# Latent attention: the norm in its own block, three groups projected at once, raw copies and GpSimd roots

## The reference, cut to what matters

```python
xn = layernorm(x, ln_x_g, ln_x_b); ln = layernorm(latents, ln_l_g, ln_l_b)   # x: context, latents: layernorm(x)
q = (ln @ Wq)...; kv = concatenate([xn @ Wkv, ln @ Wkv], axis=1)             # 16 heads of 64
qn = rmsnorm(q, qn_g) * scale; kn = rmsnorm(k, kn_g)
sim = einsum('bhid,bhjd->bhij', qn, kn); ... masked; attn = softmax(sim)
out = einsum('bhij,bhjd->bhid', attn, v) ... @ Wout + bout
x = x + tanh(g) * out
```

## Time and profile before

| | us |
|---|---|
| median of 3 runs | 1561.75 (1558.82 to 1564.23) |
| profiled execution, its own time | 1560.97 |
| its span | 1558.9 |
| TensorE busy | 1319.1 (85%), mean granted clock 0.926 |
| VectorE, ScalarE, GpSimd busy | 833.6 (53%), 688.5 (44%), 490.2 (31%) |
| latent attention, start to first exponential | 472.4 to 550.34 |

### The profile page before, as it was taken

One profiled execution on the slowest core, in us unless ns is written; L12 is line 12 of the kernel. 1 busy time (PEld: TensorE's weight loads), 2 busy tenths in 40 slices (PEclk: granted clock), 3 DMA queues, 4 the chain that ended last, 5 costly groups with the idle time before them and its releaser, 6 DMA issues. The chain is left out here.

```text
span 1558.9 us, 19760 instructions
## 1 busy us (share of the span) xinstructions
PE 1319.1 (85%) x7007; PEld 574.6 (37%) x7007; DVE 833.6 (53%) x1386; ACT 688.5 (44%) x1153; POOL 490.2 (31%) x471
## 2 busy tenths in 40 slices
PE   5779687759966699999999999999959976677998
PEld 2214222238952233333333333333326752222443
DVE  3757666362344566655665666566364434632554
ACT  3354434422225256655665666465433434254222
POOL 1013201066610144453553444445416750010000
PEclk9999899769977899999999999999979997797999
DMA  8500400249531000000000000000041123000340
GB/s 229 223 1 0 109 17 1 94 145 381 212 97 60 0 1 1 1 0 1 1 0 1 1 1 0 1 0 1 1 145 40 53 73 114 0 1 1 77 102 13
DMA packets 44267, 85.73 MB, mean 55 GB/s; under 512 B 7646, under 2 KB 27230, under 8 KB 43422
## 3 DMA queue, kind: packets, MB, share of 16 engines
q1 hardware_dynamic: 30124, 70.44, 13.9%
q0 software_dynamic: 4544, 9.32, 2.1%
q10 hardware_dynamic: 9504, 4.72, 1.1%
HBM read 76.56 MB, written 11.04 MB: 56 GB/s over the span
## 5 line engine op out<-in xcount | busy, mean ns | idle before, releaser
L2456 ACT ACTIVATE a_prob<-a_TP 128x512 f32<-128x512 f32 x256 | 138.9, 595 | 121.0 <-PE a_TP L2287 119.2
L2541 DVE TENSOR_REDUCE a_lat<-a_SP 128x2 f32<-128x1024 f32 x128 | 156.0, 1218 | 59.1 <-PE a_SP L2256 59.1
L2652 POOL TENSOR_TENSOR a_acc<-a_prob 128x512 f32<-128x512 f32 x64 | 79.8, 1267 | 303.1 <-ACT a_prob L2456 303.1
L2283 PE MATMUL a_TP<-a_qn,a_kn 64*128 64x512 f32 x512 | 148.0, 642 | 2.9 <-ACT a_prob L2456 2.9
L2298 PE MATMUL a_MS<-a_prob,a_V 128*64 128x512 f32 x512 | 122.7, 599 | 0.2 <-ACT a_prob L2456 0.2
L3109 DVE TENSOR_REDUCE a_nm<-a_A 128x8 bf16<-128x616 f32 x84 | 67.0, 797 | 50.6 <-PE a_A L2829 50.4
L3287 POOL TENSOR_TENSOR a_on<-a_osb,a_rden 128x512 f32<-128x512 f32 x9 | 11.4, 1271 | 242.9 <-ACT a_osb L3001 242.9
L2661 POOL TENSOR_TENSOR a_acc<-a_acc,a_prob 128x512 f32<-128x512 f32 x64 | 79.9, 1270 | 18.4 <-ACT a_prob L2456 18.4
L2656 POOL TENSOR_TENSOR a_acc<-a_acc,a_prob 77x512 f32<-77x512 f32 x64 | 80.2, 1273 | 0.0
L2283 PEld LDWEIGHTS a_TP<-a_qn,a_kn 64*128 64x128 f32 x512 | 40.6, 185 | 105.1 <-issue 75.4
L2456 ACT ACTIVATE a_prob<-a_TP,a_rowneg 77x512 f32<-77x512 f32 x64 | 40.3, 678 | 72.2 <-PE a_TP L2287 72.2
(11 more groups left out here) (493 smaller groups left out, 2854.3 us busy)
## 6 DMA issues: line engine op xcount, KB each, us to landing
ring_w<-in_F_w SPq DMA_DIRECT2D x64, 512.0 KB, 8.7
f_wide<-weight_rows SPq DMA_DIRECT2D x24, 256.0 KB, 5.7
a_maskT<-in_maskT SPq DMA_DIRECT2D x1, 2304.0 KB
a_biasT<-in_biasT SPq DMA_DIRECT2D x1, 2304.0 KB
f_b<-in_F_b SPq DMA_DIRECT2D x1, 2048.0 KB
token_rows<-f_xtok ACTq DMA_DIRECT2D x8, 256.0 KB, 5.9
a_biasQ<-in_biasQ SPq DMA_DIRECT2D x3, 616.0 KB, 5.5
ring_w<-expert_rows SPq DMA_DIRECT2D x6, 256.0 KB, 6.9
```

What stands on the lines that cost most here:

```text
L2283: nc.tensor.matmul(TP[0:n, h, :], keys(h), qn[half(h), r % 4, :], start=True, stop=False)
L2456: nc.scalar.activation(prob[0:n, 2 * k + h, :], TP[0:n, h, :], ACT.Exp, bias=rowneg[0:n, b:b + 1] if k == 0 else 0.0).then_inc(p_ready, 1)
L2541: nc.vector.tensor_reduce(lat[:, g % 2, 2 * u:2 * u + 2], SP[:, :, :], AX.X, ALU.max, negate=True).then_inc(s_used, 1)
L2652: nc.gpsimd.tensor_tensor(acc[:, h, :], prob[:, 2 + h, :], prob[:, 4 + h, :], ALU.add).then_inc(added, 1)
```

## The change

The norm is no longer a block of its own: its five pieces are part of the attention's block, in the order x of batch 0, context, x of batch 1, x of batch 2, x of batch 3, and the last two lie between later work (`centre`, `variance` on TensorE, `square_x`, `scale_x` on ScalarE, `normal` on VectorE). The loads get a semaphore each for what needs them, masks and constants before Wv and Wo. Groups 0, 1 and 2 are projected into three bank pairs (QK, TP, SP). Of groups 1 and 2 and of the context, VectorE copies the raw projection, scaled by the gain, to SBUF (`keep_raw`, `keep_context`), which frees the banks, and GpSimd multiplies by the root there (`root_raw`, `root_context`); group 0 stays as it was, and context 0 is multiplied by VectorE (`norm_context(0)`). Means of the context go to QK in place of SP, so that SP is free for the maxima. Half of the twelve value copies go to ScalarE (`keep_values`). Adding the bias to x moves to GpSimd, behind its casts.

```diff
+context = (c.ctxrep[:, :, 0:SK], cn[:, :], CW, once, 0, TP[:, 1, :], SP[:, 1, :])
+PIECES = [(c.xT[:, b * S:(b + 1) * S], c.xn[:, b * S:(b + 1) * S], S, twice, 2, TP[:, 0, :] if b == 0 else DEN,
+       SP[:, 0, :] if b == 0 else O) for b in range(B)]
+PIECES.insert(1, context)
...
+def raw_bank(g):
+    return (QK, TP, SP)[g] if g < 3 else QK
...
+def squares_of(g):
+    return V[:, 1, 2 * g - 2:2 * g, :] if g in (1, 2) else sq[:, :, :]
...
+def roots_of(g):
+    return on[:, 0:2, :] if g == 1 else rn[:, :, :]
...
-        nc.tensor.matmul(QP[:, :], Wq[:, p * P:(p + 1) * P], c.xn[:, b * S:(b + 1) * S],
+        bank = raw_bank(g)
+        nc.tensor.matmul(bank[:, 0, :], Wq[:, p * P:(p + 1) * P], c.xn[:, b * S:(b + 1) * S],
                          start=True, stop=True).then_inc(q_ready, 1)
-        if g:
+        if g >= 3:
             pe.wait_ge(k_normed, g)
-        nc.tensor.matmul(KP[:, :], Wk[:, p * P:(p + 1) * P], c.xn[:, b * S:(b + 1) * S],
+        nc.tensor.matmul(bank[:, 1, :], Wk[:, p * P:(p + 1) * P], c.xn[:, b * S:(b + 1) * S],
                          start=True, stop=True).then_inc(k_ready, 1)
...
         if i:
-            pe.wait_ge(c_normed, i)
+            pe.wait_ge(c_squared, i)
+            pe.wait_ge(c_kept, i)
...
     def mean_context(i):
+        pe.wait_ge(first_q, i + 2)
+        pe.wait_ge(first_k, i + 2)
         pe.wait_ge(c_squared, i + 1)
...
+    def first_values(i):
+        bank = (QP, KP)[i % 2]
+        if i == 0:
+            pe.wait_ge(v_in, 16)
+        if i < 2:
+            pe.wait_ge((q_normed, k_normed)[i], 1)
+        else:
+            pe.wait_ge((first_q, first_k)[i % 2], i // 2)
+        if i >= QT:
+            pe.wait_ge(c_clipped, i // 2 - 1)
...
+        dve.wait_ge(q_squared, g + 1)
+        nc.vector.tensor_scalar(qn[:, g, :], raw_bank(g)[:, 0, :], cv[:, 0:1], None,
+                                ALU.mult).then_inc(raw_kept, 1)
+        dve.wait_ge(k_squared, 2 * g + 2)
+        nc.vector.tensor_scalar(kn[:, g, :], raw_bank(g)[:, 1, :], vec[:, 5:6], None,
+                                ALU.mult).then_inc(raw_kept, 1)
...
+        dve.wait_ge(c_squared, i + 1)
+        nc.vector.tensor_scalar(knc[:, 2 * i:2 * i + 2, :], TP[:, :, 0:CW], vec[:, 5:6], None,
+                                ALU.mult).then_inc(c_kept, 1)
...
     def norm_context(i):
         dve.wait_ge(c_rms, i + 1)
-        nc.vector.scalar_tensor_tensor(out=knc[:, 2 * i:2 * i + 2, :], in0=TP[:, :, 0:B * SK],
-                                       scalar=vec[:, 5:6], in1=prob[:, 6:8, 0:B * SK], op0=ALU.mult,
-                                       op1=ALU.mult).then_inc(c_normed, 1)
+        dve.wait_ge(c_kept, i + 1)
+        nc.vector.tensor_tensor(knc[:, 2 * i:2 * i + 2, :], knc[:, 2 * i:2 * i + 2, :], c_clip(i),
+                                ALU.mult).then_inc(c_normed, 1)
...
+    def root_raw(g):
+        pool.wait_ge(ms_rms, g + 1)
+        pool.wait_ge(raw_kept, 2 * g)
+        nc.gpsimd.tensor_tensor(qn[:, g, :], qn[:, g, :], roots_of(g)[:, 0, :], ALU.mult)\
+            .then_inc(q_normed, 1)
+        nc.gpsimd.tensor_tensor(kn[:, g, :], kn[:, g, :], roots_of(g)[:, 1, :], ALU.mult)\
+            .then_inc(k_normed, 1)
...
+    nc.gpsimd.tensor_scalar(c.xT[:, :], c.xT[:, :], cv[:, 1:2], None, ALU.add).then_inc(prep, 1)
...
```

More of the change, by code:

```diff
@@ L2153, in latent_attention @@
[L2153 to L2157, removed]
+        vec_in, masks_in, prep = sem("vec_in"), sem("masks_in"), sem("prep")
+        qk_in, v_in, blk_in, o_in = sem("qk_in"), sem("v_in"), sem("blk_in"), sem("o_in")
@@ L2210, in _, with centre, variance @@
             @block.tensor
             def _(pe):
+                def centre(i):
+                    src, _, w, _, _, bank, _ = PIECES[i]
+                    if i >= 3:
+                        pe.wait_ge(n_normed, i)
+                        pe.wait_ge(ms_clipped, 3)
+                    nc.tensor.matmul(bank[:, 0:w], c.center[:, :], src, start=True, stop=True).then_inc(n_centred, 1)
+                def variance(i):
+                    w, bank = PIECES[i][2], PIECES[i][6]
+                    pe.wait_ge(n_squared, i + 1)
+                    if i >= 3:
+                        pe.wait_ge(n_logged, i)
+                        pe.wait_ge(ms_clipped, 3)
+                    nc.tensor.matmul(bank[:, 0:w], c.mean[:, :], n_sq(i)[:, 0:w], start=True,
+                                     stop=True).then_inc(n_var, 1)
@@ L2322, in output @@
                         mm.then_inc(y_ready, 1)
[L2325 to L2338 removed]
+                centre(0)
@@ new lines, in _ @@
+                centre(1)
+                variance(0)
+                centre(2)
+                variance(1)
+                variance(2)
+                pe.wait_ge(qk_in, 32)
+                pe.wait_ge(n_shifted, 1)
+                project(0)
+                pe.wait_ge(n_normed, 2)
+                project(1)
+                pe.wait_ge(prep, 4)
+                pe.wait_ge(n_normed, 3)
+                pe.wait_ge(n_logged, 3)
+                means(0)
+                project(2)
+                pe.wait_ge(ms_clipped, 1)
@@ new lines, in _ @@
+                means(1)
+                project_context(0)
+                pe.wait_ge(ms_clipped, 2)
+                means(2)
+                for i in range(4):
+                    first_values(i)
+                pe.wait_ge(blk_in, 16)
+                mean_context(0)
+                project_context(1)
+                first_values(4)
+                first_values(5)
+                mean_context(1)
+                maxima(0, 0)
+                project_context(2)
+                first_values(6)
@@ L2339, in _ @@
+                first_values(7)
+                maxima(0, 1)
+                centre(3)
+                mean_context(2)
+                maxima(0, 2)
                 project_context(3)
-                pe.wait_ge(c_clipped, 3)
+                first_values(8)
+                first_values(9)
+                variance(3)
+                maxima(0, 3)
                 mean_context(3)
[L2342 to L2358, removed]
+                centre(4)
+                first_values(10)
+                first_values(11)
+                maxima(0, 4)
+                turn(0)
                 maxima(1, 0)
-                pe.wait_ge(ms_clipped, 3)
-                turn(0)
-                pe.wait_ge(c_normed, 4)
+                pe.wait_ge(o_in, 16)
                 for r in range(R):
@@ L2444, in exponentials, with keep_values @@
+                def keep_values(i):
+                    act.wait_ge(v_ready, i + 1)
+                    if i < QT:
+                        out, src = V[:, 0, i, :], KP[:, :]
+                    else:
+                        b, j = divmod(i - QT, 2)
+                        out, src = Vc[0:SK, b, j * S:(j + 1) * S], KP[0:SK, :]
+                    nc.scalar.copy(out, src).then_inc(first_k, 1)
                 def exponentials(r, k):
@@ L2484, in _ @@
                         exponentials(r, k)
+                        if r == 0 and k == 0:
+                            scale_x(4)
                         if k == 0 and r:
@@ L2585, in _ @@
                 nc.vector.tensor_scalar(rowneg[0:SK, :], rowm[0:SK, :], -NEG, NEG, ALU.mult, ALU.add).then_inc(prep, 1)
[L2586 to L2599 removed]
+                keep_context(0)
+                clip_means(2)
+                copy_first_values(0)
+                copy_first_values(2)
+                clip_context(0)
+                keep_context(1)
+                copy_first_values(4)
+                norm_context(0)
+                clip_context(1)
+                reduce(0, 0)
+                keep_context(2)
+                copy_first_values(6)
+                reduce(0, 1)
+                clip_context(2)
+                reduce(0, 2)
+                keep_context(3)
+                copy_first_values(8)
+                normal(3)
+                reduce(0, 3)
+                clip_context(3)
+                copy_first_values(10)
+                reduce(0, 4)
                 combine(0)
+                shift(0)
                 reduce(1, 0)
[L2602 to L2603 removed]
                 for r in range(R):
```

265 lines of the change are left out of this document (192 added, 73 removed).

## The result

The changed kernel took 1543.3 us (median of 4, 1537.83 to 1547.77) against 1562.99 of the kernel before, run beside it: ratio 0.987, interval 0.9834 to 0.9906, faster by 20 us. The profiled execution's span is 1541.2 us, 17.7 less. The totals scatter by 10 to 15 us from run to run; the stage does not, so most of what follows is read from the latent attention: from its first TensorE instruction (472.45 before, 472.73 after) to its first exponential, called the opening, and the rounds behind. In the table, "last round to next stage" runs from the last round's first exponential to the next stage's first matmul, and its norm and routing from there to that stage's next barrier.

What follows compares the result with a forecast made beforehand. A chain of hand-offs bounds the opening, TensorE the rounds. Opening -21.8 us, round 0 +0.7 and TensorE's clock +1.5 sum to -19.6, giving 1541.8 us; range 1536 to 1551.

Steps and rivals of the forecast that it cites:

- the clock: Opening: TensorE partly at half clock, which the walk could not include; taken as 1.5 us, with 0 and 8 as ends.
- Rival 1: Middle of the opening: TensorE at half clock costs 8 us instead of 1.5, total 1548; chance 0.16.
- the late piece's matmul and roots: Round 0: variance(4), 0.86 us of TensorE, and scale_x(4), 1.2 us of ScalarE, delay the second exponential; 0.7 us back.
- at 5.1 us still hidden: Before round 0: GpSimd's bias add to x, taken as 2.0 us, costs no time even at its upper bound of 5.1.
- Rival 2: Opening: three VectorE instructions each wait up to a GpSimd product at the shared port, 4.2 us, total 1546; chance 0.06.
- (b): Opening before the change: three projection groups, each strictly behind the other, 10.0 us a group, raw projection's banks held throughout.
- (c): Opening before the change: twelve value projections through two banks, all copied by VectorE, 0.9 to 1.0 us each.
- (d): Opening before the change: five maxima, one after another, 1.7 to 1.9 us each.

Runs made afterwards that it cites:

- late_and_bias: Changed kernel with the third norm piece's product behind the fourth maximum and context 3's clip, bias added by VectorE in round 1; ratios to before 0.9885 and 0.9845.

## Why the prediction was right
- **The number.** 1541.8 us forecast, 1543.3 measured, with a median of before that was 1.2 us higher than the 1561.75 I started from.
- **What bounds it.** Right: hand-offs in the opening, TensorE in the rounds, which did not change by 0.05 us.
- **The opening.** I walked 56.1 us, at full clock from 476 on, and added 1.5 for the clock: 57.6. Measured 56.4, 55.5, 54.8. With the gap filled it is 54.5, so the walk was 1.6 long, and the clock cost 0.3 to 2.3 over all openings of this order (54.8 to 56.8), near its low end rather than its high one of 8. Rival 1 asked for 10 us or more at half clock beyond 490; the profiled execution has 6.8.
- **Round 0.** 0.7 us predicted, 1.7 measured (rounds 0 and 1). The part that I did price, the late piece's matmul and roots, was too dear: the second exponential came 2.97 us after the first, not 3.2, and without the bias on GpSimd the rounds lose 0.3 us, not 0.7. The step that was off: the add of the bias on GpSimd "at 5.1 us still hidden". I took 2.0 us from the nearer kind; it took 5.45, above the upper bound of 5.1, and I asked only who waits for its result, not whom it holds while it runs. Rival 2, the shared port, stood in the prediction with three VectorE instructions in the opening; none of them was held there. It came true in round 0, where I did not look, at the add of the last piece (2.24 us) and at combine of group 1 (3.48), and decided 1.4 us. When an edit moved them beside the same instruction, combine in the opening took 2.2 us more and that add 3.1.
- **The sum.** -19.6 predicted; opening and two rounds 110.9 to 91.1, 90.2 and 89.5, so -19.8 to -21.4. The opening came 1.2 to 2.8 us shorter than forecast and the rounds 1.0 longer. That these errors of opposite sign partly cancelled is luck; the mechanism of the gain is not. The profiled span shows less, 17.7, since the last round of that execution ran partly at half clock (+2.6), of which the next stage gave 1.4 back; the remaining 0.9 lie in the stages ahead and behind.
- **Where the gain sits.** In the prediction it came from (b), (c) and (d) lying beside each other. The undone parts give: norm 3.6 to 5.2 us, second bank pair 5, third about 1, values on ScalarE at most 7, roots on GpSimd at most 5. They are not independent, and the interleaving of values, contexts and maxima was never undone alone, so its share is not measured.

## What to carry to other kernels
When an opening is a chain of hand-offs with all engines half idle, write the queues side by side and walk them with durations from the trace: it gave 20 us to within 2. A further bank pair is worth what it removes from the last wait of all, here 5 us for the second and 1 for the third; try the design with one pair less. When an elementwise step is moved to GpSimd "off the path", look at what VectorE runs beside it, and at whatever that delays. Here cutting it in four and moving it to VectorE a round later both gave the 1.4 us back.

## What the runs showed of the hardware
- A VectorE add of 512 columns from SBUF took 0.49 us alone, 2.24 and 3.57 beside one GpSimd instruction of 5.45, and 0.58 beside four of 1.56. Combine (128x8) took 0.20 us alone, 0.82 to 0.89 in the later rounds, 2.35 beside the 5.45 us instruction, and 3.48 in round 0 of the changed kernel. The Trainium skill (SBUF — State Buffer, section "SBUF: two separate sides") has the port pair held for the whole instruction. The trace agrees for 2.24 and 3.57, which end 0.28 us behind GpSimd's instruction, and for an add of 1.42 beside a product of 1.49 in late_and_bias (0.29 behind). It does not for 0.58 and 2.35, which end 0.6 and 1.7 us ahead of its end, nor for 3.48, which spans three GpSimd instructions; there the measurement decides, with GpSimd's spans rough.
- GpSimd's TENSOR_SCALAR with a column of scalars took 5.45 us for 2048 columns, 2.7 ns a column, where the earlier trace rows have 1.47 us for 1536 columns, 0.96 ns. Two instructions of one name differ by 2.8 times; why is not settled.
- The last round took 26.0 or 28.5 us, and the next stage's norm and routing 39.8 or 41.3 (one of the two was long in ten of the fourteen profiles, both in none), by the moment at which TensorE's clock fell and rose. A difference of 1 to 2.5 us in such places says nothing of the code.
